# Moving one sum and three small steps of POOL, and a copy of ScalarE, within the pair loop of a fused attention and FFN kernel

## The reference

```
s   = xn + gamma * linear_attention(xn)      # per batch: Q and K with unit columns, V, tailor sum
h   = silu(q4(xn) @ q4(w_gate).T) * (q4(xn) @ q4(w_up).T)    # 704 wide
g   = silu(q4(h) @ q4(w_down).T)
out = x + s * g
```

## Time and profile before

| | |
|---|---|
| median of three runs | 637.31 us |
| profiled execution, whole | 638.52 us |
| its span | 636.7 us |
| mean granted TensorE clock | 0.973 |
| PE busy | 557.4 us, 88% |
| VectorE (DVE) busy | 566.0 us, 89% |
| ScalarE (ACT) busy | 411.6 us, 65% |
| POOL busy | 273.4 us, 43% |
| chain that ended last | PE 49%, DVE 30%, issue 12%, ACT 4%, POOL 2% |

### The profile page before, as it was taken

How to read it: one execution, slowest core, us unless ns; L and a number is a source line. 1 busy time by engine, 2 the same in 40 slices (tenths; PEclk the granted TensorE clock), 3 DMA queues, 4 the chain that set the end, 5 groups by cost and what they waited for, 6 DMA issues and landing times.

```text
span 636.7 us, 15147 instructions
## 1 busy us (share of the span) xinstructions
PE 557.4 (88%) x4957; PEld 430.2 (68%) x4957; DVE 566.0 (89%) x1201; ACT 411.6 (65%) x884; POOL 273.4 (43%) x208
## 2 busy tenths in 40 slices
PE   0267879999998998999997979999997999999776
PEld 0244657677786876678785856777885876787655
DVE  6978999989999999999898988989998999877925
ACT  3475788868677777576774767666764875654420
POOL 4453255434424454445535453543644354223216
PEclk9997999999999999999997989999997999999989
DMA  7010000000011011111101111111011110141103
GB/s 235 16 35 16 18 19 18 18 20 18 18 34 34 1 51 51 51 51 51 52 18 34 51 55 52 50 52 51 2 51 50 52 34 34 36 142 42 34 33 150
DMA packets 17474, 29.15 MB, mean 46 GB/s; under 512 B 2673, under 2 KB 4849, under 8 KB 17393
## 3 DMA queue, kind: packets, MB, share of 16 engines
q1 hardware_dynamic: 17392, 28.13, 13.3%
HBM read 19.73 MB, written 8.39 MB: 44 GB/s over the span
## 4 chain that ended last, share of the span: by engine, by line
PE 49%; DVE 30%; issue 12%; ACT 4%; POOL 2%; DVEq 1%; DMA 1%; POOLq 0%; SPq 0%; ACTq 0%
PE GU L1322 22%; PE DS L1332 6%; DVE hg L877 4%; PE G L1389 4%; DVE h L837 3%; PE DS L1334 3%; PE TR L1284 3%; DVE hq L885 3%; DVE xq L826 3%; PE GU L1342 3%; DVE ham L844 3%; DVE y L896 1%; PE TR L1300 1%; PE G L1426 1%; PE G L1404 1%
## 5 line engine op out<-in xcount | busy, mean ns | idle before, releaser
L1322 PE MATMUL GU<-wgu,xqT 128*128 128x352 f16 x1536 | 258.5, 320 | 5.7 <-DVE y L896 3.2
L1322 PEld LDWEIGHTS GU<-wgu,xqT 128*128 128x128 f16 x1536 | 150.2, 100 | 82.1 <-DVE y L896 3.5
L589 ACT ACTIVATE sil<-GU,wkap 128x352 f32<-128x352 f32 x128 | 70.9, 554 | 89.7 <-PE GU L1322 87.2
L514 POOL TENSOR_TENSOR ht<-h,hrr 128x1408 f32<-128x1408 f32 x32 | 82.8, 2589 | 81.6 <-DVE hrr L851 80.0
L837 DVE SCALAR_TENSOR_TENSOR h<-GU,wkap,sil 128x352 f32<-128x352 f32 x128 | 70.1, 547 | 32.4 <-ACT sil L589 26.4
L1332 PE MATMUL DS<-wdT,hqT 128*128 128x256 f16 x704 | 88.5, 275 | 2.6 <-ACT hqT L596 2.6
L480 POOL TENSOR_TENSOR xnat<-xs,xnat 128x510 f16<-128x510 f32 (+1 forms) x32 | 37.0, 1156 | 105.6 <-DVE ht L874 102.9
L487 POOL TENSOR_TENSOR xt<-xs,xrr 128x512 f32<-128x512 f32 x32 | 34.0, 1062 | 100.0 <-DVE hq L885 91.2
L1332 PEld LDWEIGHTS DS<-wdT,hqT 128*128 128x128 f16 x704 | 66.9, 99 | 11.6 <-ACT hqT L596 2.9
L1342 PE MATMUL GU<-Mx,xnT 128*128 128x128 f16 (+1 forms) x648 | 59.7, 234 | 3.1 <-DVE Mx L979 2.4
L885 DVE TENSOR_TENSOR hq<-hg,hs 128x704 f16<-128x704 f16 x128 | 61.0, 519 | 1.0
(11 more groups left out here) (152 smaller groups left out, 973.4 us busy)
## 6 DMA issues: line engine op xcount, KB each, us to landing
xin<-in_L_attn_x SPq DMA_DIRECT2D x34, 256.0 KB, 2.7
xe<-in_L_attn_x SPq DMA_DIRECT2D x25, 256.0 KB, 2.9
out<-o SPq DMA_DIRECT2D x25, 256.0 KB, 2.1
algebra<-in_L_ffn_w_down SPq DMA_DIRECT2D x1, 704.0 KB, 6.9
gring<-in_L_ffn_w_gate SPq DMA_DIRECT2D x1, 640.0 KB, 4.6
gring<-in_L_ffn_w_up SPq DMA_DIRECT2D x1, 640.0 KB, 5.7
xs<-in_L_attn_x SPq DMA_DIRECT2D x2, 256.0 KB, 3.9
xt<-in_L_attn_x SPq DMA_DIRECT2D x2, 256.0 KB, 4.4
```

The source lines that it names most:

```text
L514: g.tensor_tensor(paired(ht[:, 0:2 * I]), paired(h[:, q]), spread(hrr[:, q], 4 * CB), ALU.mult).then_inc(S["ht_d"], 1)
L589: a.activation(sil[:, c], GU[:, c, 0, 0:CH], ACT.Silu, scale=wkap[:, 0:1]).then_inc(S["sil_d"], 1)
L1322: last = t.matmul(GU[:, c, m, 0:CH], xqT[:, k, j, 2 * a_ + kc], wgu[:, b_, kc, 2 * m + c], start=(z == 0 and kc == 0), stop=(z == 2 and kc ...
```

## The change

Four things are moved; no instruction is added, and the arithmetic is the same.

- POOL: the order behind ht becomes x_rstd (which now waits for hw_d), x_low (which waits for the first pair of hq products, hloq 2p-1), x_divide (as before, behind the last), o.
- ScalarE: rows_out for j = 0 stands ahead of h_high instead of behind h_abs.
- VectorE: hs2 (h_parts 2) stands behind x_round 1 instead of ahead of it; the two answers squares_q and squares_k become one, at the later place (2,0,2), behind h(0,1).
- PE: in all batches but the last, high_low (four transposes that wait for VectorE's kap) is asked at (5,0,0) instead of (4,1,2), so behind the next pair's first gate_up.

```
-                (4, 1, 0): "top", (4, 1, 2): "high_low"}
+                (4, 1, 0): "top", (5, 0, 0): "high_low"}
...
+                if on["xf"]:
+                    if on["mb"]:
+                        wait(pool, "hw_d", p)
+                    x_rstd(p + 1)
+                if on["xa"]:
+                    if on["mb"]:
+                        wait(pool, "hloq", 2 * p - 1)
+                    x_low(p, k)
+                if on["xa"]:
+                    if on["mb"]:
+                        wait(pool, "hloq", 2 * p)
+                    x_divide(p, k)
                 if on["o"]:
                     e, ko = p - LAGE - 1, (k + LAGE + 1) % 2
                     wait(pool, "y_d", 4 * e + 4)
...
                         g.tensor_tensor(o[:, ko], y[:, ko], xe[:, ko], ALU.add).then_inc(S["o_d"], 1)
-                if on["xa"]:
-                    if on["mb"]:
-                        wait(pool, "hw_d", p)
-                    x_low(p, k)
-                if on["xf"]:
-                    x_rstd(p + 1)
-                if on["xa"]:
-                    if on["mb"]:
-                        wait(pool, "hloq", 2 * p)
-                    x_divide(p, k)
...
                 attention(0, 1)
+                if on["xt"] and on["m"]:
+                    rows_out(p, k, 0, on["xn"], on["e"])
                 if on["mb"]:
                     h_high(p, k)
...
                     h_abs(p)
-                if on["xt"] and on["m"]:
-                    rows_out(p, k, 0, on["xn"], on["e"])
...
-                if step == "squares_q":
+                if step == "squares":
                     wait(dve, "tq_ev", b + 1)
                     v.tensor_tensor(prod[:, :, :], t1q[:, :, :], wqT[:, :, :], ALU.mult).then_inc(S["prod_d"], 1)
-                if step == "squares_k":
...
                 if on["xb"]:
                     x_round(p, k, 0)
+                    x_round(p, k, 1)
                 if on["mb"]:
                     h_parts(p, k, 2)
-                if on["xb"]:
-                    x_round(p, k, 1)
```

More of the change, by code:

```diff
@@ L258, in build @@
                 (2, 0, 1): "t1k", (2, 1, 0): "norms", (2, 1, 2): "raw", (3, 0, 2): "tailor", (3, 1, 2): "product",
-                (4, 1, 0): "top", (4, 1, 2): "high_low"}
-        ANSWERS = {(-4, 1, 1): "own_basis", (0, 1, 0): "gram0", (1, 0, 1): "gram1", (1, 1, 0): "turn", (2, 0, 1): "squares_q",
-                   (2, 0, 2): "squares_k", (2, 1, 1): "norms", (3, 1, 0): "tailor", (4, 0, 1): "product", (4, 1, 1): "top",
+                (4, 1, 0): "top", (5, 0, 0): "high_low"}
+        ANSWERS = {(-4, 1, 1): "own_basis", (0, 1, 0): "gram0", (1, 0, 1): "gram1", (1, 1, 0): "turn", (2, 0, 2): "squares",
+                   (2, 1, 1): "norms", (3, 1, 0): "tailor", (4, 0, 1): "product", (4, 1, 1): "top",
                    (5, 0, 1): "high_low"}
@@ L268, in build @@
                     (3, 0, 2): "top", (3, 1, 1): "high_low"}
-        ANSWERS_END = {(0, 0, 2): "gram0", (0, 1, 2): "gram1", (1, 0, 1): "turn", (1, 1, 1): "squares_q", (1, 1, 2): "squares_k",
+        ANSWERS_END = {(0, 0, 2): "gram0", (0, 1, 2): "gram1", (1, 0, 1): "turn", (1, 1, 2): "squares",
                        (2, 0, 1): "norms", (2, 1, 2): "tailor", (3, 0, 1): "product", (3, 1, 0): "top", (4, 1, 2): "high_low"}
```

## The result

The changed kernel took 660.78 us (median of 4 runs, 659.36 to 663.84) against 637.41 us (4 runs, 636.89 to 638.03) for the kernel before on the same chip: a ratio of 1.037, 95% interval 1.034 to 1.041, or +23.4 us. The forecast was 657 with a range of 649 to 664.

The account below looks back on a forecast made before the run. The prediction took VectorE to bound pairs 12 to 27 and PE those from 28 on. Its terms summed to +19.7 us, +29.7 of it from late xin: 638.5 to 658.2 profiled, 657 median, range 649 to 664.

Parts of the forecast that it names:

- Q: On VectorE, the end of a pair's last h product (L885), from which the prediction times later events.
- Step 6: SP's queue: xin load waits behind the late o's store, lands 2.9 us later, statistics at Q + 5.9; +29.7 us.
- Step 5: POOL: o behind x_divide holds VectorE's hss, so hrr ends at Q + 3.17; 0.65 us where nothing covers it.
- Steps 1 to 3: POOL: o off hs, -12.2 and -0.9 us; low part off xq, -7.0; low part beside fourth h product, +10.0.
- Step 4: POOL: power and shift right behind the first rounding; first hq product waits less, -0.05 a pair, -0.8 us.
- Step 7: ScalarE: row copies ahead of h_high cost about 0.2 us each in six of pairs 2 to 8; +1.2 us.
- Step 8: High_low asked later: 2.77 us idle goes twice, -0.4 each with xin late; squares' multiplication off ht, -0.7 in loop.
- A: Rival: VectorE finds xin landed as now, so the kernel gets faster; -7.7 us, 630; chance 0.05.
- B: Rival: POOL's low part runs after the second hq pair; x_divide, o, load 1.1 us later; +5, 662; chance 0.06.
- C: Rival: VectorE's stall gives PE more idle time and PE's clock falls; +12 us, 669; chance 0.06.

Follow-up runs that it names:

- experiment 1: The changed kernel with SyncE's order altered, so the next xin load is issued ahead of the store of o: 629.61 us, ratio 0.988 to the kernel before.
- experiment 2: The kernel before with only the sum o moved behind x_divide on POOL: 656.40 us, ratio 1.029 to the kernel before.
- experiment 10: The changed kernel, SyncE's old order kept, with the sum o later still, waiting for hss: 672.91 us, ratio 1.055 to the kernel before.
- experiment 5: The kernel of experiment 1 with POOL's sum o waiting for hss up to pair 27: 625.19 us, ratio 0.980 to the kernel before.
- experiment 6: The kernel of experiment 1 with POOL's low part back beside xq, ahead of power and shift: 630.40 us, ratio 0.989 to the kernel before.
- experiment 8: The kernel of experiment 1 with the row copies back behind h_abs on ScalarE: 636.06 us, ratio 0.996 to the kernel before.
- experiment 9: The kernel of experiment 1 with high_low asked at (4,1,2) again, as before: 633.16 us, ratio 0.993 to the kernel before.

## Why the prediction was right, and where it was not

I summed the two traces by the prediction's own steps: from Q to the next statistics and from the statistics to Q over pairs 12 to 27, and what lies ahead of and behind them.

| stretch | forecast | measured (profiled) |
|---|---|---|
| Q to statistics, 16 pairs | +29.7 | +34.9 |
| statistics to Q, 16 pairs | -11.6 | -7.8 |
| ahead of the loop | +1.6 | -0.9 |
| behind it | 0 | -0.9 |
| sum | +19.7 | +25.3 |

The four misses, +5.2, +3.8, -2.5 and -0.9, partly cancel. They make 5.6 us in the profiled execution; the median lies 3.8 above the forecast.

*Step 6 (xin queued behind the store): right.* In nine of the sixteen pairs the statistics start at Q + 5.75 to 5.84 where Q + 5.9 was forecast. Experiments 1, 2 and 10 show the mechanism from three sides. The term was mis-sized by the landing: five of the sixteen loads took 3.3 to 4.3 us instead of 2.8, which adds 5.3 us, as much as the term is off. Two smaller misses nearly cancel: behind the loop's jump the statistics came 1.6 us later than before, not 0.65, and most of the other pairs came about 0.1 us early. The prediction had 3.0 as the landing's upper bound. It took this from a short stretch; the line of the whole run there has 5.7, which I put down to the start of the run, but a load of the run before at 185.80 took 3.63 us, hidden because it was issued 19.8 us ahead of its use. Its lower bound, 2.0, was misread: it belongs to a store out of the tile xin, and the shortest load of xin in that run took 2.5. The pair of the earlier trace rows took 19.8 us from Q to Q, where 18.7 was forecast: its load took 3.3 us, and its third hq product 1.49.

*Step 5 (hss held): right,* 0.87 us and hrr at Q + 3.17 as forecast; shown by experiment 5.

*Steps 1 to 3 (hs and xq free, third hq product held): right in size.* hs took 0.26 each in every pair of the loop, xq 0.41, the third hq product 1.18 in most. Two pairs lost 0.1 to 0.3 more at it. But that the low part's move "costs more than it saves" holds only where VectorE's own stretch counts; experiment 6 shows the time unchanged where PE is the other limit.

*Step 4 (power and shift): the gain of 0.05 a pair was not there.* hq starts 0.03 us behind hg with POOL idle too. The rule of the Trainium skill (SBUF — State Buffer, "Who interferes with whom") is not tested by the changed kernel, where rs is all but over when xq starts (445.59 + 0.71 against 446.22). In experiment 6, with the low part ahead of rs again, the rows are those of the earlier trace rows: rs runs from 424.05 to 424.94 (0.89 us instead of 0.71), and hg, begun beside it at 424.63, takes 1.61 us, as it does with POOL idle. So for this power the rule does not hold there either.

*What the forecast of -11.6 missed.* The x rounding's second part now stands directly behind the first, which it reads. It starts 0.72 us behind it, where hs, which does not read it, started 0.60 behind it before (256.50 and 257.10): 0.12 a pair, 2 us in the loop. And ScalarE's hT comes 0.82 us late in two pairs of the loop, 1.6 us. With the 0.8 us of step 4 that is 4.4, a little more than the 3.8 that are missing. Timeline of VectorE in the changed kernel, then its idle time ahead of L877 by what ended it (us, times):

```profile
461.85 0.69 DVE L820 SCALAR_TENSOR_TENSOR xt<-xT,xt 128x512 f32<-128x512 f32 x1
462.57 0.69 DVE L823 SCALAR_TENSOR_TENSOR xg<-xT,xt 128x512 f16<-128x512 f32 x1
```
```profile
  ACT hT L641: 3.5, 6
```

*Step 7 (row copies): wrong, and in sign.* I counted what the copies delay on ScalarE, +1.2 us, and did not ask who waits for them. PE did: in the kernel before it idled 1.59 us ahead of L1284 in pair 12 and 0.95 to 1.3 in three more pairs of the loop, and 10.6 us for xnT in all, by this line of its waits:

```profile
PE TR L1284 <- ACT xnT L602: 10.6, 9, 2.5
```

Experiment 8 measured -6.5 us where xin is in time. In the changed kernel it seems to show only outside the loop, as the -0.9 and -0.9 of the table against the forecast +1.6 and 0; experiment 8's 2.5 and 1.8 us there fit.

*Step 8 (high_low): right.* "-2.1 each" for two pairs stands against 3.6 us in experiment 9. In the changed kernel, where xin is late, -0.5 each is left (Q + 5.75 instead of Q + 6.29), where -0.4 was forecast. The squares' multiplication takes 0.68 us in the loop instead of 1.04, the forecast 0.7 for two.

*The rivals.* A described the kernel with xin in time: 630, and experiment 1 measured 629.6. Some of that agreement is luck: by its trace VectorE's stretch from the statistics to Q saved 7.0 us of the 11.6, 4.6 too few, while the other three stretches came out 5.4 us better than A had them. B: the release took what it had taken before; the low part always ran first. C: the granted clock was 0.977 against 0.973, and its lower level was there for 32 us of the run against 36: PE's longer idle times did not bring more of it.

## What to carry to other kernels

When an instruction is moved later, follow its result to the queue that takes it away, and list what that queue issues next: here a store that nothing yet waited for held back a load that the busiest engine needed, at 30 us, and putting the load first gave it all back. Count for each moved step both who is delayed behind it and who was waiting for it; only the first was counted for the row copies, and the sign came out wrong. Edits do not add where the limit changes between them: the same wait for hss was worth -4.4 us in one queue order and +11 to +12 in the other.

## What the runs showed of the hardware that was not expected

A load of 256 KB issued behind a store usually lands in 2.8 us, but at times in 3.3 to 4.3. The DMA views of the changed kernel over seven microseconds, first around the load at 294.9, then around the one at 536:

```profile
q1 hardware_dynamic: 432, 0.79, 30.3%
q8 instruction: 1, 0.02, 1.4%
...
xin<-in_L_attn_x SPq DMA_DIRECT2D x1, 256.0 KB, 4.3
```
```profile
q1 hardware_dynamic: 432, 0.79, 33.4%
...
xin<-in_L_attn_x SPq DMA_DIRECT2D x1, 256.0 KB, 2.8
```

In the slow case one packet of 16 KB of the instruction queue started at 295.99, amid the load's own packets, and took 1.60 us. In all five slow loads such a packet (8 or 16 KB, 0.96 to 1.60 us) started between 0.4 us before and 1.3 us after the load's issue; in the other eleven none of more than 0.31 us did. Other traces fit less well. In experiments 2 and 10 ten of 32 loads of xin in the loop took over 3.1 us. Two of them (3.19 and 3.26) had no such packet, and for the longest, 4.72 us at 506.86 in experiment 2, the packet came only 2.0 us behind the issue. No load with such a packet between 0.4 us before and 1.3 us after its issue landed in under 3.3 us there. That program code shares the 16 engines with the data and delays the last packets of a load is thus likely for some of the slow loads, but it does not account for all; no experiment took it away, and it stays open.
